# Local attention with TensorE transposes, and with VectorE blocks and DMA round trips in their place

## The reference, cut to what matters

```python
h = shift_token(x)                      # second half of the channels one token late
q, k, v = split(h @ wqkv)               # 8 heads of 64
q, k = l2norm(q) * qs, l2norm(k) * ks   # then rotated (rotary_xpos)
sim = 8 * q @ [k_before, k_own].T       # windows of 128 queries, 256 keys, masked
o = softmax(sim) @ [v_before, v_own]    # 128 x 512
x = x + o @ wo
h = layernorm(shift_token(x))
a, g = split(h @ w1 + b1)
x = x + (a * gelu(g)) @ w2 + b2
```

## Time and profile before

| | |
|---|---|
| runs, median (lowest, highest) | 5243.1 us (5241.11, 5250.66) |
| profiled execution, span | 5235.6 us |
| the profiled execution's own time | not printed beside the span; the lowest timed run is 5.5 us above the span and the median 7.5 us |
| TensorE matmuls busy | 4795.1 us (92%) |
| VectorE, ScalarE, GpSimd busy | 3521.7 (67%), 3087.6 (59%), 2288.2 us (44%) |
| SyncE's DMA queue | 863248 packets, 297.62 MB, 24.3% of 16 engines |

### The profile page before, as it was taken

The page is one execution under the profiler, slowest core; times in us unless marked ns, Lnnn a source line. Parts: engine busy times, 40 slices in busy tenths (PEclk is TensorE's granted clock), DMA queues, the critical chain, the costliest instruction groups (busy, mean ns, idle before and its releaser), DMA issues. The chain is left out here.

```text
span 5235.6 us, 274484 instructions
## 1 busy us (share of the span) xinstructions
PE 4795.1 (92%) x111000; PEld 4080.3 (78%) x111000; DVE 3521.7 (67%) x10729; ACT 3087.6 (59%) x8362; POOL 2288.2 (44%) x3065
## 2 busy tenths in 40 slices
PE   7988888588888887679999999999999999999999
PEld 6888888588888886557877777777877777777777
DVE  5666666488888884756666666666666666666665
ACT  5777777344444443556666666666666665666655
POOL 1222222377777772034444444444444444444443
PEclk8999999699999997889999999999999999999999
DMA  2433333477777775910000000000100000000000
GB/s 82 101 87 94 96 91 93 122 168 165 166 164 164 165 163 154 298 55 16 16 14 16 15 16 12 16 16 16 50 23 22 18 22 20 20 22 18 22 20 17
DMA packets 914892, 373.14 MB, mean 71 GB/s; under 512 B 645840, under 2 KB 875984, under 8 KB 913616
## 3 DMA queue, kind: packets, MB, share of 16 engines
q1 hardware_dynamic: 863248, 297.62, 24.3%
q10 hardware_dynamic: 51392, 73.02, 4.7%
HBM read 209.12 MB, written 161.35 MB: 71 GB/s over the span
## 5 line engine op out<-in xcount | busy, mean ns | idle before, releaser
L2291 ACT ACTIVATE l_prob<-l_prob,l_nb,l_rq 128x256 f32<-128x256 f32 x1024 | 604.6, 592 | 275.6 <-DVE l_nb L2077 275.4
L1942 POOL TENSOR_TENSOR l_pn<-l_prob,l_rinv 128x512 f32<-128x512 f32 x512 | 532.5, 1040 | 331.7 <-DVE l_rinv L2057 326.5
L2487 PE MATMUL lD<-l_hid,w 128*128 128x128 f32 x3072 | 388.2, 275 | 20.8 <-DVE l_hid L2132 20.8
L2487 PEld LDWEIGHTS lD<-l_hid,w 128*128 128x128 f32 x3072 | 364.1, 192 | 23.4 <-DVE l_hid L2132 23.2
L2275 ACT COPY l_qT<-lA 128x512 f32<-128x512 f32 x128 | 74.9, 585 | 413.9 <-PE lA L2395 413.9
L1097 POOL TENSOR_TENSOR sc_aqx<-sc_late,sc_headmask 128x256 f32<-128x256 f32 x256 | 172.7, 675 | 275.6 <-PE sc_Y L1190 272.7
L1173 PE MATMUL sc_AB<-sc_aq,sc_bkx 32*32 32x32 f32 x16384 | 256.6, 198 | 38.2 <-POOL sc_bkx L1097 29.3
L1949 POOL TENSOR_TENSOR l_x1s<-l_x 128x128 f32<-128x128 f32 x128 | 58.0, 453 | 493.8 <-DVE l_x L2115 493.6
L497 POOL TENSOR_TENSOR rk<-rk,bkraw 128x256 f32<-128x256 f32 x64 | 54.6, 871 | 477.8 <-DVE bkraw L383 477.8
L1115 POOL TENSOR_TENSOR sc_bkT<-sc_tok,sc_headmask 128x128 f32<-128x128 f32 x512 | 261.7, 531 | 0.0
L2479 PE MATMUL lA<-l_hn,w 128*128 128x128 f32 x2048 | 259.8, 281 | 2.0 <-POOL l_hn L1960 2.0
(11 more groups left out here) (291 smaller groups left out, 15151.0 us busy)
## 6 DMA issues: line engine op xcount, KB each, us to landing
scratch_cm<-cm SPq DMA_DIRECT2D x64, 512.0 KB, 4.1
sc_early<-scratch_cm ACTq DMA_DIRECT2D x59, 512.0 KB, 4.5
scratch_tok<-vt SPq DMA_DIRECT2D x512, 48.0 KB, 1.8
scratch_part<-sc_att SPq DMA_DIRECT2D x64, 384.0 KB, 4.4
sc_part<-scratch_part SPq DMA_DIRECT2D x64, 384.0 KB, 4.1
sc_tok<-scratch_tok ACTq DMA_DIRECT2D x62, 384.0 KB
l_h<-scratch_h SPq DMA_DIRECT2D x128, 129.0 KB, 2.6
scratch_gr<-gr SPq DMA_DIRECT2D x64, 256.0 KB
```

Source lines behind the costliest of these rows:

```text
L1942: tt(pn[s][:, pair], prob[s][:, pair], rinv[s][:, pair].unsqueeze(2).broadcast_to([P, 2, 2 * P]), ALU.mult).then_inc(Q["pn"][s].sem, 1)
L2291: last_ = nc.scalar.activation(prob[s][:, h], prob[s][:, h], ACT.Exp, scale=rq8[s][:, h:h + 1], bias=nb[s][:, h:h + 1], accum_out=sums[s][ ...
L2487: last_ = mm(bank[s][3][:, c * P:(c + 1) * P], w2[:, m, c * P:(c + 1) * P], hid[s][:, m], start=(c == 0 and m == 0), stop=(c == CC - 1 and ...
```

## The change

- P: GpSimd normalises a pair in place. VectorE transposes it in blocks of 32x32 (`turn_p`, 128x512 a pair) into `pb`. When all four pairs (eight heads) are there, SyncE writes `pb` to a DRAM scratch (`write_p`, 128 x 8 KB = 1 MB) and reads it back with four DMAs (`read_p`), each of which fills 32 partitions of `pT` in runs of 2 KB. The 16 TensorE transposes and the four copies out of PSUM go.
- q and k: the same with one 128x512 block transpose, a write of 256 KB and four reads of 64 KB each in runs of 512 B (`write_q`, `read_q`, `write_k`, `read_k`). The 8 TensorE transposes and the two PSUM copies go. `add_q` moves from VectorE to GpSimd.
- `values`, `head_out`, `project_out`, the layer norm and the MLP of a unit move out of its half into the next one, which belongs to the other stream. In TensorE's list `values` of pairs 0 and 1 now stand first in the half, ahead of `scores`.
- `head_out` is two ScalarE copies of 128x256 where it was four of 128x128 on VectorE, ahead of `exponent` in ScalarE's list; the `rq8` scaling and `carry` move to ScalarE too.
- The next unit's `project` is that of the same stream, in the order k, v, q.
- `qT`, `kT` and `pT` have new layouts: consecutive queries of one head pair lie 4 elements apart in `qT`, and `kT` and `pT` hold runs of 32 elements.

The diff, cut to its core (removed lines of the old lists are left out where the new list is shown whole; each `sem_inc` on a free counter is left out as well):

```diff
+        pb, pT = two("pb", [P, BL, 2, NHP, 2, 32]), two("pT", [P, BL, 2, NHP, 2, 32])
+        oT = two("oT", [P, NHP, P])
...
-            return ((u - 1, 1 - w), (u, w)) if s == 0 else ((u, w), (u + 1, 1 - w))
+            return (u - 1, 1 - w) if s == 0 else (u, w)
...
+        def valued(s, hp):
+            return bank[s][(3, 1)[hp // 2]][:, hp % 2 * P:(hp % 2 + 1) * P]
...
+        def write_q(s, u):
+
+            sp.wait_ge(S["q_turned"][s].sem, S["q_turned"][s].after(u))
+            sp.wait_ge(S["qT"][s].sem, S["qT"][s].after(u, 1))
+            sp.dma_start(a["qz"][s], q1[s][:].rearrange("p h d -> p (h d)")).then_inc(S["q_out"][s].sem, 16)
+
+        def read_q(s, u):
+            sp.wait_ge(S["q_out"][s].sem, S["q_out"][s].after(u))
+            sp.wait_ge(Q["sc"][s].sem, Q["sc"][s].after(u * NHP - 1))
+            for j in range(BL):
+                sp.dma_start(qT[s][32 * j:32 * j + 32].rearrange("p (i t) h -> p i (t h)", i=BL),
+                             a["qz"][s].rearrange("(i c) (j n) -> j c i n", i=BL, j=BL)[j]).then_inc(S["qT"][s].sem, 16)
...
+        def write_k(s, u):
+            sp.wait_ge(S["k_turned"][s].sem, S["k_turned"][s].after(u))
+            sp.wait_ge(S["kT"][s].sem, S["kT"][s].after(u, 1))
+            sp.dma_start(a["kz"][s], k1[s][:].rearrange("p h d -> p (h d)")).then_inc(S["k_out"][s].sem, 16)
...
+        def write_p(s, u):
+
+            sp.wait_ge(Q["p_turned"][s].sem, Q["p_turned"][s].after(u * NHP + NHP - 1))
+            sp.wait_ge(H["pT"][s].sem, H["pT"][s].after(u, 1))
+            sp.dma_start(a["pz"][s], pb[s][:].rearrange("p j g h x t -> p (j g h x t)")).then_inc(H["p_out"][s].sem, 16)
+
+        def read_p(s, u):
+            sp.wait_ge(H["p_out"][s].sem, H["p_out"][s].after(u))
+            sp.wait_ge(Q["pv"][s].sem, Q["pv"][s].after(u * NHP - 1))
+            for j in range(BL):
+                sp.dma_start(pT[s][32 * j:32 * j + 32].rearrange("p i g h x t -> p i (g h x t)"),
+                             a["pz"][s].rearrange("(i c) (j n) -> j c i n", i=BL, j=BL)[j]).then_inc(H["pT"][s].sem, 16)
...
+        def half(s, u, w, l, mlp=True):
+            o = 1 - s
+            um, wm_ = partner(s, u, w)
+            un, wn = um + 1, 1 - wm_
+            fin = not isinstance(u, int) or u > 0
+            if within(un):
+                read_q(o, un)
+            if fin and not layer(u - 1, l):
+                store(s, u - 1, 0)
+            if at(s, u, 1, NW):
+                sp.wait_ge(S["w2_ps"][1].sem, S["w2_ps"][1].after(NW - 1))
+                sp.dma_start(w2[:], a["w2"][1]).then_inc(sems["w2"], 16)
+            if s == 1 and within(u + 2):
+                load_rot(u + 2, w, layer(u + 2, l))
+            if mlp and within(um + 2):
+                if isinstance(um, int) and um + 2 == NW:
+                    sp.wait_ge(sems["zero"], 16 * NB)
+                load_window(o, um + 2, wm_, layer(um + 2, l))
+            if mlp and layer(um, l):
+                load_xa(o, um)
+            if at(s, u, 0, NW):
                 sp.wait_ge(S["wo_ps"][1].sem, S["wo_ps"][1].after(NW - 1))
                 sp.dma_start(wo[:], a["wo"][1]).then_inc(sems["wo"], 16)
+            if within(un):
+                write_k(o, un)
+                read_k(o, un, wn)
+            write_p(s, u)
+            read_p(s, u)
+            if fin and layer(u - 1, l):
+                store(s, u - 1, 1)
+            if at(s, u, 1, NW - 2):
+                sp.wait_ge(S["q_ps"][1].sem, S["q_ps"][1].after(NW - 1))
+                sp.dma_start(wqkv[:], a["wqkv"][1]).then_inc(sems["wqkv"], 16)
+            if within(u + 1):
+                write_q(s, u + 1)
...
+        def turn_q(s, u):
+
+            dve.wait_ge(S["qr"][s].sem, S["qr"][s].after(u))
+            nc.vector.transpose(q1[s][:].rearrange("p h d -> p (h d)").rearrange("p (j t h) -> p h j t", j=BL, h=NHP),
+                                qr[s][:].rearrange("p h d -> p (h d)").rearrange("p (h j c) -> p h j c", h=NHP, j=BL)
+                                ).then_inc(S["q_turned"][s].sem, 1)
+
+        def turn_k(s, u):
+            dve.wait_ge(S["kr"][s].sem, S["kr"][s].after(u))
+            nc.vector.transpose(k1[s][:].rearrange("p h d -> p (h d)").rearrange("p (j h t) -> p h j t", j=BL, h=NHP),
+                                kr[s][:].rearrange("p h d -> p (h d)").rearrange("p (h j c) -> p h j c", h=NHP, j=BL)
+                                ).then_inc(S["k_turned"][s].sem, 1)
...
+        def turn_p(s, u, hp):
+
+            n = u * NHP + hp
+            g, at = hp // 2, 2 * (hp % 2)
+            dve.wait_ge(Q["pn"][s].sem, Q["pn"][s].after(n))
+            if hp == 0:
+                dve.wait_ge(H["p_out"][s].sem, H["p_out"][s].after(u, 1))
+            nc.vector.transpose(pb[s][:, :, g, at:at + 2].rearrange("p j h x t -> p (h x) j t"),
+                                prob[s][:, 2 * hp:2 * hp + 2].rearrange("p h (x j k) -> p (h x) j k", x=2, j=BL)
+                                ).then_inc(Q["p_turned"][s].sem, 1)
...
+        def half(s, u, w, l, mlp=True):
             o = 1 - s
+            um, wm_ = partner(s, u, w)
+            un = um + 1
+            fin = not isinstance(u, int) or u > 0
+            lm, lp = layer(um, l), layer(u - 1, l)
+            if fin:
+                add_out(s, u - 1, 1 - w, lp)
+            if within(un):
+                norm_k(o, un)
             row_max(s, u, w, 0)
+            if fin and lp:
+                scale_out(s, u - 1)
+            row_max(s, u, w, 1)
+            row_max(s, u, w, 2)
+            inverse_sums(s, u, 0)
+            row_max(s, u, w, 3)
+            if mlp:
+                attended(o, um, wm_)
+            inverse_sums(s, u, 1)
+            inverse_sums(s, u, 2)
             if mlp:
                 deviate(o, um, wm_)
             inverse_sums(s, u, 3)
+            turn_p(s, u, 0)
+            turn_p(s, u, 1)
+            if within(un):
+                turn_k(o, un)
+            turn_p(s, u, 2)
+            turn_p(s, u, 3)
+            if within(u + 1):
+                sum_k(s, u + 1)
+                sum_q(s, u + 1)
+                rotate_q(s, u + 1, 1 - w)
+                clamp(s, u + 1)
             if mlp:
+                gate(o, um, 0, lm)
+                gate(o, um, 1, lm)
+            if within(u + 1):
+                turn_q(s, u + 1)
             if mlp:
+                gate(o, um, 2, lm)
+            remask(s, u, w)
...
+        def head_out(s, u, g):
+
+            act.wait_ge(Q["pv"][s].sem, Q["pv"][s].after(u * NHP + 2 * g + 1))
+            act.wait_ge(S["wo_ps"][s].sem, S["wo_ps"][s].after(u, 1))
+            nc.scalar.copy(oT[s][:, 2 * g:2 * g + 2].rearrange("p h t -> p (h t)"), bank[s][(3, 1)[g]][:, 0:2 * P]
+                           ).then_inc(O["oT"][s].sem, 1)
...
+        def half(s, u, w, l, mlp=True):
             o = 1 - s
+            um, wm_ = partner(s, u, w)
+            un, wn = um + 1, 1 - wm_
+            if mlp:
+                carry(o, um, wm_)
+                head_out(o, um, 0)
+                head_out(o, um, 1)
             exponent(s, u, 0)
+            exponent(s, u, 1)
+            exponent(s, u, 2)
+            exponent(s, u, 3)
             if mlp:
                 square_dev(o, um)
+            if within(un):
+                copy_v(o, un, wn)
+            if within(u + 1):
+                square_k(s, u + 1)
             if mlp:
                 inverse_std(o, um)
+            if within(u + 1):
+                square_q(s, u + 1)
             if mlp:
                 gelu(o, um, 0, layer(um, l))
                 gelu(o, um, 1, layer(um, l))
                 gelu(o, um, 2, layer(um, l))
+                act.preload_act_table_set(LN_EXP)
+            if within(u + 1):
+                inverse_norms(s, u + 1)
...
+        def values(s, u, hp, l):
+            g, at = hp // 2, 2 * (hp % 2)
+            if hp == 0:
+                pe.wait_ge(H["pT"][s].sem, H["pT"][s].after(u))
...
+        def half(s, u, w, l, mlp=True):
             o = 1 - s
+            um, wm_ = partner(s, u, w)
+            fin = not isinstance(u, int) or u > 0
+            drained = within(um + 1)
+            if mlp:
+                values(o, um, 0, layer(um, l))
+                values(o, um, 1, layer(um, l))
+            scores(s, u, w, 0)
+            scores(s, u, w, 1)
+            if fin and layer(u - 1, l):
+                turn_out(s, u - 1)
+            if mlp:
+                values(o, um, 2, layer(um, l))
+                values(o, um, 3, layer(um, l))
+            scores(s, u, w, 2)
+            scores(s, u, w, 3)
+            if mlp:
+                reloaded("wo", o, um)
+                project_out(o, um)
+            if within(u + 1):
+                reloaded("wqkv", s, u + 1)
+                project(s, u + 1, 1 - w, 1)
             if mlp:
                 mean(o, um)
+            if within(u + 1):
+                project(s, u + 1, 1 - w, 2)
             if mlp:
                 variance(o, um)
```

(46 more changed lines are left out.)

450 lines of the change are left out of this document (163 added, 287 removed).

## The result

The changed kernel takes 6026.9 us (median of 4 runs, 6024.1 to 6029.3) against 5242.4 (5241.1 to 5250.7) beside it on the same chip. The ratio is 1.149, with a 95% interval of 1.148 to 1.151. The forecast was 5823 us, range 5400 to 6150.

The account below looks back on a forecast made before the run. TensorE's list was taken to bound the old kernel, one chain through P's DRAM trip the new: terms of 25.8 us plus 1.6 for the clock give 27.4 us a half, 127 periods plus start and end 5823 us, range 5400 to 6150.

Parts of the forecast that it names:

- 1 and the clock: From `pT` landing to the exponents: `values`, scores and `head_out`, 3.7 us, plus 1.6 us for TensorE's lower clock.
- 2 to 4: Four exponents 4.7 us, `inverse_sums` of pair 3 0.5 us, then VectorE's block transposes at 0.68 us each; P turned at 12.3.
- Term 7: `read_p`, P's 1 MB read from DRAM in four issues, taken as 4.9 us.
- Terms 5 and 6: SyncE's k round trip, 2.7 us, and four issues, 2.4 us, before `write_p`; then P's 1 MB write, 4.9 us.
- The queue: On SyncE, turned P waits behind k's round trip; `write_p` is issued 3.7 us after P is ready.
- The clock: TensorE's idling before `pT` lands drops it to 1.2 GHz, slowing the first matmuls on the chain by 1.6 us.
- term 1: `values` and scores on TensorE and ScalarE's `head_out`, from `pT` landing to the exponents, 3.7 us with handovers.
- That `write_q` costs nothing: `write_q` on SyncE lies behind `read_p`; q is needed a whole period later, so it costs nothing.
- The 3.6 us taken off TensorE's list: The 24 transposes leaving each half were taken at 3.6 us, shrinking TensorE's list to 19.0 us.
- The floor of 20.3 us: With a short round trip, the MLP's tail, `out` until 20.3 us, would keep the period from falling under about that.
- the first rival: Faster: P's round trip hides, TensorE's list and the MLP's tail set a 20.3 us period, 4921 us; chance 0.06.

Follow-up runs that it names:

- `h_one`: Changed kernel with P read back by one 1 MB DMA in 128 runs of 8 KB, blocks landing permuted; 5800.3 us, ratio 1.107.
- `a_wide`: Changed kernel with each of the four reads of P filling all 128 partitions in 2 KB runs, blocks landing permuted; 5858.8 us, ratio 1.119.
- `b_qlate`: Changed kernel with the write of q held back until `pT` has landed; 5983.3 us, ratio 1.142.
- `c_korder`: Changed kernel with SyncE's order write k, write P, read k, read P; 5632.2 us, ratio 1.075.
- `d_warm`: Changed kernel plus 24 matmuls without use at the end of TensorE's list, while it waits; 5870.8 us, ratio 1.121.
- `o_vwide`: `n_vlast` with the P reads of `a_wide`, so P lands permuted; 5058.7 us, ratio 0.965.
- `k_defer`: Changed kernel with scores and exponents before `values` and `head_out`, MLP work cleared around P's transposes, `write_p` before `write_k`, `out` one half later; 5669.7 us.
- `n_vlast`: `m_early` with v's projection moved to the end of TensorE's list; 5195.6 us, ratio 0.991.
- `e_first`: Changed kernel with all scores ahead of all `values` in TensorE's list and `head_out` behind the second exponent; 5755.0 us, ratio 1.098.
- `m_early`: `k_defer` with k normed and rotated in its projecting half, k's round trip before P is turned, `values` between scores 1 and 2; 5256.3 us.

## Why the prediction was right, and where its sizes were off

The direction and the mechanism hold; the time was 204 us low. The first `values` start at 2323.0 and the last at 6003.2, 127 periods of 28.98 us, against 2311 and 27.4. So the period gives +200 us, the start +12, the tail -1 (24.3 us), and the 7 us that I added outside the span gives -7.6: the median lies 0.6 us below the profiled span. Of the start's 12 us, 8 are the earlier stages: the window loads begin at 2264.0 in this execution and at 2256.2 in the one before, and the change doesn't touch what lies ahead of them.

Means of 8 halves from 3000 us on (their period is 28.7), beside the steps:

| step | predicted | measured |
|---|---|---|
| `values` to the first exponent (1 and the clock) | 5.3 | 5.7 |
| exponents, sums, three transposes (2 to 4) | 7.2 | 7.5 |
| `write_k` to `write_p` (5) | 5.1 | 4.15 |
| `write_p` to `read_p` (6) | 4.9 | 4.1 |
| `read_p` to `values` (7) | 4.9 | 7.4 |

- **Term 7 is the one that was mis-sized**, by 2.5 us a half. I took it near a single transfer of 1 MB between the earlier trace rows's 512 KB and 1536 KB. `h_one`, which is such a transfer, needs 5.3, close to the 5.15 between those rows. The four narrow reads need 7.4: `a_wide` puts 1.1 on the narrow cut, and the step from `a_wide` to `h_one` 0.7 to 1.0 on four issues with shorter runs in place of one. Both differ from the changed kernel also in where blocks land. `b_qlate` puts 0.3 on q's write. The rule in "SBUF — State Buffer", section "Door 1: The DMA port swizzle" of the Trainium skill, which I had weighed and left out of the sum, pointed the right way, and my estimate from that page was 5.5. It doesn't account for the 7.4 by itself, as the four reads of `a_wide`, at full width, still need 6.3.
- Terms 5 and 6 were too high: k's 256 KB is read 2.2 us after its write, not 2.7, and the four issues take 1.73 us, not the 2.34 of the earlier trace rows. P's 1 MB was written in 4.1 us. Together 1.8 us. Errors of opposite sign thus took two thirds of the one in term 7 out of the total, and the time came as near as it did by that luck.
- **The queue**, that P waits behind k on SyncE, was right: 3.2 us against 3.7, and `c_korder` gives back 3.1.
- **The clock** was right in kind and somewhat low in size: 1.6 us were forecast from the earlier trace rows, and `d_warm` gives 2.2 for halves without it (5.9 to 3.7), of which 1.7 came back on the mean. The 3.7 us of term 1 at full clock are what those halves take.
- The block transpose costs 675 ns, the price of a 128x512 operation as in the earlier trace rows.
- That `write_q` costs nothing was wrong by 0.3 us a half.
- The 3.6 us taken off TensorE's list were too many. `o_vwide`, at a clock of 0.98 from 2400 to 3700 us, is busy for 1234 of these 1300 us at 21.4 us a half, a list of 20.3 us and not 19.0. About 2.5 us went, which is the 2.6 from start to start. It didn't touch the time, as the list isn't the bound. The new layouts of q and k cost 0.1 us for the scores of two pairs (1.24 in `d_warm` at full clock, 1.12 before).
- The floor of 20.3 us for a hidden round trip was too low for this order of the lists. `k_defer` doesn't wait for P and needs 26.2 us a half: the boundary chain wasn't in the forecast. Yet the first rival, that the trip can be hidden, is true of another order: `n_vlast` beats the kernel before.

TensorE is busy 77% in the stretch, where I wrote near 70%: the list is longer than I took it, and part of it runs at the lower clock.

## What to carry to other kernels

When an operation between two engines is replaced by a trip through DRAM, price the chain from landing to landing and not the engine that is relieved, and count what stands ahead of the trip in the queue that issues it: one swap of two calls was 3.1 of the 6.1 us that a half had lost. A bound that is removed uncovers the next at once (`e_first`, `k_defer`, `n_vlast` each moved the wait to another line), so read after each step which releaser ends TensorE's idle time. A long round trip is paid for by work that can stand between issue and use, and the last 1.9 us of such work were placed by looking for the one hole left.

## What the runs showed of the hardware

- A block transpose whose output has a stride of 4 elements takes 1.11 us, where those with runs of 32 take 0.67. VectorE's groups of the changed kernel from 3000 to 3500 us:

```profile
L2189 DVE STREAM_TRANSPOSE l_pb<-l_prob 128x512 f32<-128x512 f32 x68 | 43.3, 675 | 0.0
L2139 DVE STREAM_TRANSPOSE l_q<-l_qr 128x512 f32<-128x512 f32 x18 | 20.0, 1111 | 0.0
L2145 DVE STREAM_TRANSPOSE l_k<-l_kr 128x512 f32<-128x512 f32 x17 | 11.4, 669 | 0.0
```

- Four 256 KB reads that fill the same 1 MB take 7.1 to 7.4, 5.9 to 6.3 or 13.7 us to their use, by how they are cut: 32 partitions each, 128 partitions each, or 128 partitions from a source with an outermost dimension of 4. The first two ranges are of two kernels each (the changed one and `n_vlast`, `o_vwide` and `a_wide`).
- The length of the wait just before doesn't tell the clock by itself. In `m_early` 1.55 us at one boundary are followed by `values` of 1.80 us, and 1.63 us at the next by 1.09:

```profile
3333.57 0.57 PE L2486 MATMUL lB<-l_kT,l_qT 64*128 64x256 f32 x1 [1.63 <-issue]
...
3335.14 1.09 PE L2504 MATMUL lD<-l_pT,l_V 128*64 128x128 f32 x16 [0.26 <-DMA l_pT<-scratch_pz]
```
